# Half-tile score matmuls taken in turn with transposes in a decoder layer with cross-attention

## The reference, cut to what matters

```python
def _L0_xattn_ref(input_Q, input_K, input_V, attn_mask, W_Q, b_Q, W_K, b_K, W_V, b_V, W_out, b_out):
    NUM_HEADS = 16; D_K = 64; D_V = 64
    Q = (input_Q @ W_Q.T + b_Q).reshape(batch, -1, NUM_HEADS, D_K).transpose(0, 2, 1, 3)
    K = (input_K @ W_K.T + b_K)...
    V = (input_V @ W_V.T + b_V)...
    scores = jnp.einsum('bhqd,bhkd->bhqk', Q, K) / np.sqrt(D_K).astype(np.float32)
    scores = jnp.where(attn_mask[:, None, :, :], jnp.float32(-10000.0), scores)
    attn = jax.nn.softmax(scores, axis=-1)
    out = jnp.einsum('bhqk,bhkd->bhqd', attn, V)
    return out.transpose(0, 2, 1, 3).reshape(batch, -1, NUM_HEADS * D_V) @ W_out.T + b_out
x = x + _L0_xattn_ref(_layernorm(x), ctx_1024, ctx_1024, mask, ...)
```

## Time and profile before

| what | value |
|---|---|
| median of 3 runs | 1489.99 us (1489.0 to 1493.08) |
| the profiled execution | 1488.46 us |
| its span, first to last instruction | 1486.7 us |
| TensorE matmuls busy | 1398.3 us (94% of the span) |
| VectorE busy | 1114.5 us (75%) |
| GpSimd busy | 904.2 us (61%) |
| ScalarE busy | 875.3 us (59%) |
| TensorE's granted clock, mean of the span | 0.981 |

### The profile page before, as it was taken

How to read it: one execution, slowest core, us unless ns; L and a number is a source line. 1 busy time by engine, 2 the same in 40 slices (tenths; PEclk the granted TensorE clock), 3 DMA queues, 4 the chain that set the end, 5 groups by cost and what they waited for, 6 DMA issues and landing times. The chain is left out here.

```text
span 1486.7 us, 29684 instructions
## 1 busy us (share of the span) xinstructions
PE 1398.3 (94%) x10217; PEld 1341.1 (90%) x10217; DVE 1114.5 (75%) x2887; ACT 875.3 (59%) x1643; POOL 904.2 (61%) x970
## 2 busy tenths in 40 slices
PE   7789999999999999999999999999999999967785
PEld 5689999999999999999999999999999999956674
DVE  6667787878787777777777877787878786759565
ACT  5556565656565665565565656565656565646453
POOL 2566566666666666666666666666666676534353
PEclk9899999999999999999999999999999999988998
DMA  4334251423233242414141413131313121035212
GB/s 125 83 104 126 74 150 45 127 62 113 70 87 103 66 130 63 126 50 135 50 126 53 134 46 119 49 117 50 117 50 114 40 79 37 20 98 169 78 55 90
DMA packets 164810, 131.20 MB, mean 88 GB/s; under 512 B 79189, under 2 KB 158822, under 8 KB 164150
## 3 DMA queue, kind: packets, MB, share of 16 engines
q1 hardware_dynamic: 160228, 122.78, 29.3%
q0 software_dynamic: 3360, 5.47, 1.2%
q10 hardware_dynamic: 1074, 1.05, 0.2%
HBM read 96.08 MB, written 38.34 MB: 90 GB/s over the span
## 5 line engine op out<-in xcount | busy, mean ns | idle before, releaser
L1474 ACT CAST pT_hi<-banks 128x512 fp32r<-128x512 f32 (+1 forms) x672 | 358.5, 538 | 411.4 <-PE banks L1642 400.8
L1533 DVE TENSOR_TENSOR pT_lo<-banks,pT_hi 128x512 fp32r<-128x512 f32 (+1 forms) x576 | 356.4, 625 | 226.6 <-ACT pT_hi L1474 222.4
L1417 POOL TENSOR_SCALAR probs<-probs,row_inv 128x1408 f32<-128x1408 f32 x192 | 278.0, 1448 | 244.7 <-DVE row_inv L1586 242.1
L1410 POOL TENSOR_SCALAR bias<-mask,c_all 128x1444 f32<-128x1444 uint8 (+1 forms) x208 | 306.5, 1474 | 119.3 <-DVE nmax L1521 77.6
L1642 PE MATMUL banks<-ident,probs 128*128 128x128 f32 (+1 forms) x2304 | 365.5, 274 | 3.7 <-POOL probs L1419 2.8
L1674 PE MATMUL banks<-pT_hi,ctx_hi 128*128 128x256 f32 (+1 forms) x1056 | 327.8, 310 | 5.1 <-DVE ctxT_lo L1553 5.1
L1465 ACT ACTIVATE probs<-probs,nmax 128x1448 f32<-128x1448 f32 x192 | 289.7, 1509 | 36.0 <-DVE nmax L1521 34.7
L1674 PE MATMUL banks<-pT_hi,ctx_lo 128*128 128x256 f32 (+1 forms) x1056 | 302.4, 286 | 0.0
L1674 PE MATMUL banks<-pT_lo,ctx_hi 128*128 128x256 f32 (+1 forms) x1056 | 301.8, 286 | 0.0
L1642 PEld LDWEIGHTS banks<-ident,probs 128*128 128x128 f32 (+1 forms) x2304 | 269.9, 140 | 18.7 <-DVE pT_lo L1533 7.2
L1624 PE MATMUL banks<-ctxT_hi,qh 128*128 128x362 f32 (+1 forms) x832 | 239.9, 370 | 2.9 <-PEq L623 2.8
(11 more groups left out here) (320 smaller groups left out, 2081.3 us busy)
## 6 DMA issues: line engine op xcount, KB each, us to landing
mask<-mask_dram SPq DMA_DIRECT2D x192, 180.5 KB, 2.4
q_dram<-stage SPq DMA_DIRECT2D x96, 200.0 KB, 3.0
nat<-in_ctx SPq DMA_DIRECT2D x16, 704.0 KB
qh<-q_dram SPq DMA_DIRECT2D x14, 800.0 KB, 5.0
ql<-q_dram SPq DMA_DIRECT2D x14, 800.0 KB, 6.7
mask_dram<-in_mask_BxSxS_bk SPq DMA_DIRECT2D x32, 141.0 KB, 2.7
up_raw<-in_L_ffn_W SPq DMA_DIRECT2D x32, 128.0 KB, 2.3
q_dram<-stage SPq DMA_DIRECT2D x32, 100.0 KB, 2.0
```

Of the source, the lines that this page charges most:

```text
L1410: pool.tensor_scalar(bias[(t + b) % 2][0:n, 0:SK], masks[s][0:n, :], MASKED, c_all[0:n, b, t:t + 1], ALU.mult, ALU.add).then_inc(bias_read ...
L1417: pool.tensor_scalar(prob(j)[0:n, 0:FIRST], prob(j)[0:n, 0:FIRST], rinv[0:n, s:s + 1], 1.0, ALU.mult, ALU.mult)
L1474: act.copy(pT_hi[tslot(b, j)][:, 0:w], banks[:, T_BANK + j % 2, 0:w]).then_inc(turned_hi, 1)
L1533: dve.tensor_tensor(p_lo, turn, p_hi.bitcast(F32), ALU.subtract).then_inc(turned_lo, 1)
```

## The change

Where a score of the half tile stands directly ahead of a step in the list, and that step has four plain transposes (not the first or last of its group), the score is left out at its own place. TensorE then does the step's values as before, and after them the score's six matmuls and the step's four transposes in turn: one score matmul, one transpose, four times, and two score matmuls. This is so for score 24 with step 25 and score 25 with step 26 in batches 1 to 15, and for score 25 with step 26 in batch 0: 31 places. The waits of both (the banks of the score, the banks of the transposes) stand ahead of the first score matmul. The transposes signal after the fourth, the score after the sixth.

```diff
+def half_tiles():
+    return {n for n in range(len(ORDER) - 1)
+            if ORDER[n][0] == "score" and ORDER[n][2] >= 2 * FT and ORDER[n + 1][0] == "step"
+            and ORDER[n + 1][1] < NB and STEPS[ORDER[n + 1][2]][0] < NG - 1
+            and 0 < STEPS[ORDER[n + 1][2]][1] < KT - 2}
...
+                def half_and_turn(b, n, tb, j):
+                    i, half, (g, k0) = b % 2, n % 2, STEPS[j]
+                    rows = slice(FT * 128, FT * 128 + HALF)
+                    wait(pe, scores_taken, 2 * NT * b + n - 1)
+                    wait(pe, turned_lo, NSTEP * tb + j - 1)
+                    passes = ((qh, ctxT_hi[i]), (qh, ctxT_lo[i]), (ql, ctxT_hi[i]))
+                    for a in range(6):
+                        qpart, kpart = passes[a // 2]
+                        c = 2 * half + a % 2
+                        last = pe.matmul(banks[0:HALF, S_BANK + c, 0:CW], qpart[:, i, rows],
+                                         kpart[:, c * CW:(c + 1) * CW], start=a < 2, stop=a >= 4)
+                        if a < 4:
+                            k, t = k0 + a // 2, tiles_of(g)[a % 2]
+                            turn_last = pe.transpose(banks[:, T_BANK + j % 2, a * 128:(a + 1) * 128],
+                                                     prob(t)[:, k * 128:(k + 1) * 128], ident[:, :])
+                        if a == 3:
+                            turn_last.then_inc(turned, 1)
+                    last.then_inc(scores_ready, 1)
...
-                for kind, b, j in ORDER:
+                for n, (kind, b, j) in enumerate(ORDER):
                     if kind == "step":
                         jj, bb = lagged(j, b)
                         if bb >= 0:
                             values(bb, jj)
-                        if b < NB:
+                        if n - 1 in HALF_TILES:
+                            half_and_turn(*ORDER[n - 1][1:], b, j)
+                        elif b < NB:
                             turn(b, j)
+                    elif n in HALF_TILES:
+                        pass
                     elif kind == "score":
                         score(b, j)
```

More of the change, by code:

```diff
@@ L157 @@
 ROUNDS, GROUPS = shared_banks()
+def half_tiles():
[3 more added lines that the diff above has]
+            and 0 < STEPS[ORDER[n + 1][2]][1] < KT - 2}
+HALF_TILES = half_tiles()
 ROUTE_LATE = {
```

## The result

The changed kernel took 1500.41 us in the median of 4 runs (1498.4 to 1500.68), beside 1489.61 for the kernel before in the same comparison (1489.0 to 1493.08, 4 runs). The ratio, which weighs all the runs, is 1.0065 with an interval of 1.005 to 1.0079, that is 9.7 us slower, between 7.4 and 11.8; the two medians alone lie 10.8 apart. The forecast was 1499, 9.1 us slower. The profiled execution took 1500.40 with a span of 1498.7.

What follows compares the result with a forecast made beforehand. The prediction saw TensorE held once a batch at step 30 by a chain over VectorE, ScalarE and GpSimd without room; 16 x 0.57 = 9.1 us on 1489.99 gave 1499, range 1492 to 1504 (the forecast's own 1495 to 1503).

Steps and rivals of the forecast that it cites:

- The mix costs nothing and saves nothing: TensorE, 31 places: score matmuls and transposes in turn cost 0, bounded by 0.44 saved a mix and 0.48 lost a batch.
- Rival A: TensorE: the mix hides weight loads, 0.22 saved a mix; 1492, no change; chance 0.12.
- rival B: TensorE: each added turn from transposes costs 0.08, 0.48 a batch on top; 1507; chance 0.08.
- Score 25 is 0.57 late on VectorE: VectorE starts score 25 at 609.35 in place of 608.78, after 0.49 of old room is used up.
- score 24's 0.17: VectorE starts score 24 at 607.46, 0.17 late; the prediction said this does not decide.
- the four value matmuls' 0.13: Expectation for e2: score 25 late on TensorE by four value matmuls, 0.47, so 0.13 late on VectorE; 2 us slower.
- Nothing in the chain gives it back: From VectorE's score 25 over ScalarE and GpSimd to TensorE's step 30 no room; the whole 0.57 is lost each batch.
- Rival C: The chain does not hold step 30 in most batches, or earlier transposes and values swallow the delay; 1484 to 1491; chance 0.08.
- The covers: TensorE's mixes begin only 0.25 to 0.3 after the splits they wait for; without this room loss would come on top.
- The ranking matmuls wait, inside the same loss: TensorE waits 0.3 to 0.5 there for the outputs' lower half, time it would have stood at step 30 anyway.
- The sum: 16 batches x 0.57 = 9.1 us, added to the median 1489.99, gives 1499.
- the expectation for e6: Step 30 no longer waits, only the ranking matmuls, about 0.3 in 15 batches; near 1491, 4 to 5 above e5.

Runs made afterwards that it cites:

- e1: Against the changed kernel: no turns, the score in a block of six behind the values and the four transposes; 1499.76 against 1491.2 for the kernel before.
- e2: As e1, but with the score's block ahead of the four transposes; 1493.79 us against 1491.2 for the kernel before.
- e4: Against the changed kernel: only score 25 in turn with transposes, score 24 as before; 1500.94 us against 1491.2 for the kernel before.
- e3: Against the changed kernel: only score 24 in turn with transposes, score 25 as before; 1494.09 us against 1491.2 for the kernel before.
- e6: Changed kernel with the half tile's reciprocal ahead of the split of step 27; 1493.9 us against 1490.7 for the kernel before.
- e5: Kernel before with the half tile's reciprocal ahead of the split of step 27 on VectorE; 1485.59 us against 1490.7 for the kernel before.
- e7: As e6, with the lower half of the outputs of steps 18 to 23 ahead of score 25; 1493.0 us against 1490.03 for the kernel before.

## Why the prediction was right

- *The mix costs nothing and saves nothing:* right. A pair takes 0.28, and e1 without turns takes the same time. Rival A fell (a transpose before a load of 64 columns took 0.11 in the mix too), and rival B fell: the longer first score matmul after a transpose, now at every turn, is an earlier start.
- *Score 25 is 0.57 late on VectorE:* right to the hundredth, 0.567 a period, and 0.37 + 0.20 = 0.57 where TensorE pays it in batch 6. Its start is 0.15 after TensorE's last matmul in the changed kernel, e1, e2 and e4. The smaller terms stood too: score 24's 0.17 became 0.18 in e3, the four value matmuls' 0.13 became 0.133 in e2.
- *Nothing in the chain gives it back:* right. 4.67 from score 25 to the reciprocal, before and after. Rival C fell. One link beside the chain did have room: the outputs' lower half, which I put 0.57 later, follows score 25 by 615.58 - 614.08 = 1.50 in place of 610.47 - 608.78 = 1.69, so that it came only 0.38 later. The sum does not rest on it.
- *The covers:* the mix's own waits for the splits of two steps ahead never showed; TensorE has no idle row ahead of either mix.
- *The ranking matmuls wait, inside the same loss:* right, 0.37 is lost there in batch 6, within the 0.3 to 0.5 worked out, and step 30 pays the rest.
- *The sum:* 8.50 in 15 periods and about 0.6 in batch 0 make the 9.1 forecast; the comparisons gave 9.7 and 8.3 by their ratios, each within the other's interval. That the median came within 1.4 of 1499 is in part luck, since head and tail alone moved by 2.6 between two executions of the changed kernel; what bears the prediction out are the 15 periods.
- Where I was wrong: the expectation for e6. The step that failed was to take step 30 and the ranking matmuls for the only places at which TensorE meets the late chain. It meets it at step 32 as well, as it did in the kernel before (0.17 in the row shown under e5), and e7 showed the loss move there.

## What to carry to other kernels

On an engine that is busy throughout, moving a piece later need not cost anything on that engine (here a pair took 0.28 either way), and its price is read from the engine that takes the result: the delay, plus the time to start after a wait, minus the room in which the taker was busy with other work. Then follow the taker's chain to the next place where the busy engine waits for it; if there is one without room in each period, the rest of the delay is lost in each period. Freeing that place only helps as far as the next one does not wait on the same chain, so shortening the chain itself (e5) was worth more than any of the orders of matmuls tried here.

## What the runs showed of the hardware

- Transposes (0.11) and score matmuls (0.17) taken one by one cost the sum of both, although the weights alternate between 64 and 128 columns at each instruction. A matmul behind a transpose is put down 0.03 after it and shows 0.08 longer; the time is not lost.
- VectorE, standing in a wait for a score, started 0.15 after the last matmul's end as the profile models it, in all five traces whose rows are shown (before, changed, e1, e2, e4).
- The profile names the routing instruction L481 as releaser of the ranking matmuls. By the code they wait for the step `choose`, an instruction done long before, and for the outputs' lower half (L1603, ending at 615.58 + 0.41 = 615.99 in the changed kernel). With that one moved ahead in e7 the wait went. L481 came earlier in e7 as well, so it is the code that tells the two apart: the name in brackets was only the event nearest in time.
